# One kernel for a decoder layer with a routed FFN: where the slot-table writes of a tile stand

## What is computed

```
x = x + xattn(layernorm(x), ctx, ctx, mask, ...)   # 16 heads, 257 context rows per batch, softmax
x = x + attn(layernorm(x), Wqkv, Wout, ...)        # causal linear attention (elu + 1), then a norm
x = x + ffn(layernorm(x), gate_w, shared_*, expert_*)

# ffn, per token:
shared = silu(x @ shared_wg.T) * (x @ shared_wu.T) @ shared_wd.T
scores = sigmoid(x @ gate_w.T)                      # 64 experts
topw, topi = top_k(scores, 8);  topw = topw / topw.sum(-1)
# token -> slot `pos` of expert `topi` ; out = sum over its 8 experts of topw * expert(x)
```

## Time and profile before

| | us |
|---|---|
| Median of three runs | 1292.09 (1290.09 to 1292.49) |
| The profiled execution | 1304.77 |
| Its span, first to last instruction | 1302.8 |
| Mean granted clock of TensorE | 0.986 of full speed |
| PE busy in the span | 1228.3 (94%) |
| DVE busy | 742.7 (57%) |
| ACT busy | 593.8 (46%) |
| POOL busy | 393.7 (30%) |

### The profile page before, as it was taken

One profiled execution on the slowest core, in us unless ns is written; L12 is line 12 of the kernel. 1 busy time (PEld: TensorE's weight loads), 2 busy tenths in 40 slices (PEclk: granted clock), 3 DMA queues, 4 the chain that ended last, 5 costly groups with the idle time before them and its releaser, 6 DMA issues. The chain is left out here.

```text
span 1302.8 us, 32014 instructions
## 1 busy us (share of the span) xinstructions
PE 1228.3 (94%) x9830; PEld 926.2 (71%) x9831; DVE 742.7 (57%) x1645; ACT 593.8 (46%) x1184; POOL 393.7 (30%) x312
## 2 busy tenths in 40 slices
PE   5999999999999999999998879999999999999993
PEld 5888787887877878878775436667677676667671
DVE  4345665746747657566456735655555565655550
ACT  2443443433434434334341154656655666655651
POOL 0001011030020110300203233465554656746542
PEclk9999999999999999999999989999999999999997
DMA  6632100210101102101021176999999999999886
GB/s 232 274 125 35 62 26 19 69 36 28 60 18 56 31 18 69 36 27 52 10 64 67 41 253 205 328 294 345 298 319 305 282 323 330 366 283 314 261 240 105
DMA packets 67369, 205.44 MB, mean 158 GB/s; under 512 B 16063, under 2 KB 18495, under 8 KB 56912
## 3 DMA queue, kind: packets, MB, share of 16 engines
q1 hardware_dynamic: 43392, 159.78, 34.0%
q0 software_dynamic: 23888, 44.40, 16.1%
HBM read 177.32 MB, written 37.03 MB: 165 GB/s over the span
## 5 line engine op out<-in xcount | busy, mean ns | idle before, releaser
L453 POOL TENSOR_TENSOR rstd<-vep,half 128x1 f32<-128x1 f32 x32 | 20.7, 647 | 557.2 <-DVE vep L628 557.2
L969 PE MATMUL bank<-ch,wkh 128*128 128x256 f32 x512 | 157.6, 308 | 10.6 <-DVE cl L647 7.0
L553 ACT ACTIVATE kt<-bank,colb 128x256 f32<-128x256 f32 x128 | 60.5, 473 | 223.8 <-PE bank L971 223.8
L1640 PE MATMUL ebank<-guh,xth 128*128 128x512 f32 x380 | 154.8, 408 | 1.2 <-DVE xtl L1534 0.8
L1529 DVE TENSOR_TENSOR gul<-wgu,guh 128x2048 fp32r<-128x2048 f32 x54 | 123.8, 2293 | 53.9 <-ACT guh L1445 46.7
L1374 POOL DMA_INDIRECT xg<-xn_rows,ig x95 | 123.8, 1303 | 94.8 <-issue 66.6
L1642 PE MATMUL ebank<-guh,xtl 128*128 128x512 f32 x380 | 149.0, 392 | 0.0
L1641 PE MATMUL ebank<-gul,xth 128*128 128x512 f32 x380 | 148.3, 390 | 0.0
L970 PE MATMUL bank<-cl,wkh 128*128 128x256 f32 x512 | 145.4, 284 | 0.0
L971 PE MATMUL bank<-ch,wkl 128*128 128x256 f32 x512 | 145.3, 284 | 0.0
L1670 PE MATMUL ebank<-wd,ht 128*128 128x512 f32 x292 | 134.3, 593 | 0.8 <-ACT ht L1430 0.8
(11 more groups left out here) (242 smaller groups left out, 2468.8 us busy)
## 6 DMA issues: line engine op xcount, KB each, us to landing
wgu<-in_egu SPq DMA_DIRECT2D x54, 1024.0 KB
wd<-in_edn SPq DMA_DIRECT2D x54, 512.0 KB
sgu<-in_egu SPq DMA_DIRECT2D x17, 1024.0 KB
craw<-in_ctx SPq DMA_DIRECT2D x32, 514.0 KB, 3.3
sdn<-in_edn SPq DMA_DIRECT2D x17, 512.0 KB
wqkv<-in_wqkv SPq DMA_DIRECT2D x1, 3072.0 KB, 18.3
second_sums<-x1b SPq DMA_DIRECT2D x9, 256.0 KB, 4.2
xa<-in_x SPq DMA_DIRECT2D x8, 256.0 KB, 2.9
```

The lines of the kernel that those rows point to most:

```text
L969: mm(out, wkh[:, c, w], h[:, c, :], start=c == 0, stop=False)
L1640: mm(out, ah[:, c, :], bh[:, c, :], start=c == 0, stop=False)
```

## The change

In the passes, each write first waits until PE has finished the block before its own: `s_kv` counts finished blocks over all tiles, `6 * (BT * t + b) + k` of them lie ahead of block (t, b, k). `tick` only serves waits on a register's value. In the tail, tile 6's first three writes (`PACED = 8 - 1 - 4`) stay at its pos step; one each then waits for tile 7's steps v, A3, DEN1 and NUM1 to be written by PE (`px_wait`), and the eighth for tile 7's outproj, ahead of that step's two roots. The eight writes of tile 7 itself (`EARLY`) stay as they were.

```diff
+PACE = ("v", "A3", "DEN1", "NUM1")
+PACED = K - 1 - len(PACE)
...
                 if front and WRITE <= s < WRITE + K:
+                    wait(pool, s_kv, 6 * (BT * t + b) + k, tick)
                     write(s - WRITE)
...
                 if n == "outproj":
+                    if type(t) is int and t == NT - 1:
+                        px_wait(pool, n, t)
+                        write(K - 1)
                     root(norm_post(t, 1))
                     root(norm_post(t, 2))
                 if n == "pos" and type(t) is int and t >= NT - 2:
                     table_ready(t)
-                    for j in range(EARLY if t == NT - 1 else K):
+                    for j in range(EARLY if t == NT - 1 else PACED):
                         write(j)
+                if n in PACE and type(t) is int and t == NT - 1:
+                    px_wait(pool, n, t)
+                    write(PACED + PACE.index(n))
```

## The result

The changed kernel takes 1296.04 us (median of nine runs, 1294.99 to 1298.01), the kernel before 1292.09 us (nine runs beside them, 1290.09 to 1293.24). The ratio is 1.0029, with a 95% interval of 1.0020 to 1.0038: slower by 4 us. The forecast was 1291.6 us and no change, its range 1279 to 1295.

The account below looks back on a forecast made before the run. PE, busy 94%, was taken to bound the kernel. Its 13.5 us of holds were taken as a recording cost, so the plain run was forecast at 1292.09 - 0.5 = 1291.6 us, range 1279 to 1295.

Parts of the forecast that it names:

- What bounds the kernel: Reading of the profile: PE, busy 94%, is the bound; it loses time beside table-write bursts in passes and last tile.
- These holds: PE's delays beside bursts of eight table writes: at q and k in passes 2 to 7, and in the last tile.
- The sum of 13.5 us: All holds in the profiled execution: 5 x 1.74 + 0.97 + 3.8 us, 1.0% of it.
- The 1.74 us a pass: Extra length of a pass with table writes over one without: 86.75 against 85.01 us, 1.50 of it at q and k.
- What of it is in a plain run: Step taking the holds as a cost of recording PE beside a burst; plain gain between 0 and 13.5, set at 0.5 us.
- The second reason: Argument from the holds' shape: in passes they stand at q and k, called PE's densest records, 128 in 7.3 us.
- The change part by part: Step placing each paced write; passes 2 to 7 were to lose their hold, -9.7 us in the profiled execution.
- rival B: Lone writes cost PE more than a burst: 27 x 0.22 = 5.9 us, so 1298 us; chance 0.08.
- The last tile: Term for the last tile's burst: 3.8 us lost, 3 to 3.8 recovered, 3.4 taken off; write ahead of the roots free.
- The profiled execution: Forecast for the profiled run of the changed kernel: 1304.77 - 9.7 - 3.4 = about 1291.7 us.
- Rival A: The holds exist in plain runs too: 1279.0 us if all go, 1283 to 1288 if recording lengthened them; chance 0.32.
- Rival C: Pacing leaves bursts, holds only halve: profiled 6 us less, plain 1292 or 1286; no separate chance, inside the 0.60.

Follow-up runs that it names:

- two_fours_tail: two_fours plus the change's five last-tile waits; 1292.42 us on a slow chip, 0.9898 of the kernel before.
- tail_again: The kernel of tail_only, unchanged, run again on a slow chip: 1300.99 us, 0.9967 of the kernel before.
- two_fours: Kernel before with one wait a pass: writes 4 to 7 form a second burst after the second batch's 64 small products; 1296.67 us, slow chip, ratio 0.9932.
- before_again: The kernel before, unchanged, profiled a second time, on a slow chip: median 1309.34 us, 1.0017 of itself.
- waits_free: passes_only with all eight waits of a pass on the first one's value, so the writes burst again; 1292.99 us, fast chip, ratio 0.9995.
- tail_only: The change with only its five last-tile waits, passes as in the kernel before; 1293.37 us on the fast chip, ratio 1.0006.
- passes_only: The change with only the waits of passes 2 to 7, last tile as in the kernel before; 1296.15 us, fast chip, ratio 1.0026.
- av_shift: passes_only with write 4 waiting until PE is through with the 64 small attention products; 1291.66 us, fast chip, 0.9995 of the kernel before.
- aimed: Kernel before with each pass's writes in three groups (3, 3, 2) released to start beside the 64 small products; 1299.89 us, fast chip, ratio 1.0056.
- after_third: The changed kernel, unchanged, run again on a slow chip: 1306.07 us, 1.0006 of the kernel before.
- after_again: The changed kernel, unchanged, run and profiled again on a slow chip: 1305.66 us, 0.9989 of the kernel before.
- mended: The changed kernel with write 4 of a pass waiting for the end of the 64 small products; 1298.88 us, slow chip, 0.9947 of the kernel before.

## Why the prediction was wrong

**What bounds the kernel.** Right in where the time stands: pass length, q and k beside the burst, the last tile. These holds are real in that profile. The sum of 13.5 us was well sized too: two_fours_tail, which removes them, gains 12.4 and 13.4 us on slow chips. The 1.74 us a pass were a little high: tail_again and two_fours, on one chip, are 86.80 - 85.33 = 1.47 us apart, and the other 0.3 us stand in every profile.

**"What of it is in a plain run": this step failed.** I set 12.68 us between profile and median beside 13.5 us of holds and took the holds for a cost of recording. The near agreement was true, the cause was not. The kernel before has the holds on a slow chip, where its profiled execution is as long as the others (before_again: profile 1307.83 in runs around 1309). Its bursts of eight have no hold on the fast chip though they are recorded (waits_free and tail_only), and one kernel, tail_only and tail_again, has the holds on one chip and not on the other, profiled both times. So recording is not enough to make them. The profile has a slow chip's time and holds, the median the fast one's. The second reason was misread as well: q and k are not "the place with the densest records of PE". The trace of before has 64 products and their 64 loads in 0.78 us, nine times as dense, and it was never asked what a write beside them would do:

```profile
295.56 0.78 PE L1019 MATMUL bank<-att,vb 128*32 128x32 f32 x64
```

The rule that I cited from the Trainium skill (page "NOTIFIC — the notification-queue block", section 7.1, producers held back by recording) explains nothing here: the profiled execution is no longer than the other runs on either kind of chip. For the fast chip the conclusion, nothing to gain from the holds, was still right.

**"The change part by part", the passes: this step made the sign wrong.** I placed write 4 near 293.5 and put its price for PE at nothing without a reason; that it might cost was left to rival B, at 0.08. It came at 294.62, 0.22 us into the 64 small products, and I had not asked what PE does at that moment. The row was there: 295.56 in the trace before, less the 1.5 us of hold, is 294.06, within the 0.96 us of a write that starts at 293.5. A wait on "block 11 done" releases the write just when the densest instructions of the pass start. The sum had no term for this. Measured on the fast chip: 2.5 us longer products in passes_only (27.3 for 24.8) and in the change, beside losses of 3.1 us in the runs of passes_only (2.1 to 4.7 by its interval) and 3.95 of the change (2.6 to 4.9). The pass length holds somewhat more: 0.53 us a pass over tail_only in passes_only, 0.47 in the change (from 191.56 to 534.82 in four passes), which makes 3.2 and 2.8 us in six. The last microsecond of the change is within its interval, and no row holds it. av_shift and aimed show the cause from both sides: 0 meetings, no loss; 18 meetings, 7.5 us in the runs and as much in the row's busy time.

**The last tile.** Right on a slow chip: 3.9 us gained (tail_again) for the 3.8 us of hold that were read and the 3.4 that were taken off. Worth nothing on the fast chip (tail_only), so the 4.1 us between the two profiles are mostly the chips'. The write ahead of the roots costs nothing (2.04 us between DVE and root, 2.05 before).

**The profiled execution.** I expected 1291.7 us, it took 1297.61. On a fast chip this says nothing of the holds, which are not there at all.

**The rivals.** Rival A (the holds are real) fits the slow chips: the profiles of two show the holds, and on the third the kernel without them is 13.4 us faster. Yet the change gains nothing clear there, since write 4 and write 7 give back at the small products (4.7 + 2.7 us) and beside the A products (5.6 us of idle time for 1.0, in after_third) what the bursts no longer take. Rival B had the right sign and the wrong mechanism: not every lone write costs (0.22 us times 27), but, on the fast chip, the one that starts beside the small products (0.4 to 0.5 us times 6). So the right sign of rival B is luck as far as its reason goes. Rival C is refuted: writes 0 to 3 stayed a burst, and the hold at q and k went all the same (after_again).

## What to carry to other kernels

Before a wait is put on another engine's progress, ask what that engine starts at that very moment: a release point at the end of a block is the beginning of the next one. Here an indirect DMA of POOL cost nothing beside the matmuls of 512 columns, cost on each chip where it was tried when it started inside a run of small ones, and cost on slow chips also beside the A products, whose result DVE then took late. Splitting the burst at such places, four writes and four, was safe in this kernel; whether it is the number or the place that makes it safe was not separated. And when a profiled execution and the median differ by 1%, run the same kernel once more, with its profiled and its timed runs on one chip, before any theory is built on the difference.

## What the runs showed of the hardware that was not expected

- Chips differ by 1% on the same kernel, with nearly the same granted clock (0.986 to 0.991 in every profile of the study): 1292 to 1293 us on one, 1305 to 1307 on three. Most of it, if not all, is the behaviour beside POOL's indirect DMAs; with these placed well (two_fours_tail) a slow chip takes 1292.4 us and 85.33 us a pass, the fast one 85.35 (tail_only). What that kernel takes on the fast chip stays open.
- On slow chips, beside eight indirect writes in 10 us, DVE gets q 3.8 us late (7.42 us of idle time in before_again for 3.67 in after_again) and the products of q and k take 1.5 us longer. Bursts of four before q and k and beside v hold nothing (two_fours), but the third of three writes beside the A products delays PE by some 0.8 us a pass (mended). So it is not the number alone.
- 64 products of 32 columns, which take 0.78 us, take 1.30 us on the fast chip and 2.1 us on a slow one with an indirect write beside them. A memset on POOL or a DMA issued by SP at the same place changes nothing.
- The same kernel measured against itself on a slow chip gave 1.0017 with an interval that leaves out 1. Differences of that size need a row of the trace behind them.
